# Cross-attention in one core: one doubled column block more, a different order ahead of the batch loop, row loads of 512 KB

## What is computed

```python
qp = x @ Wq + bq; kp = ctx @ Wk + bk; vp = ctx @ Wv + bv
w = softmax(qp @ kp.T / sqrt(512), axis=-1)
a = w @ vp
gate = concat(qp, a) @ Wg + bg
out = (a * mask) * sigmoid(gate) + x
```

## Time and profile before

| | us |
|---|---|
| runs of the kernel (3) | 432.0, 435.47, 435.5 |
| median | 435.47 |
| the profiled execution | 433.39 |
| its span, first to last instruction | 431.5 |

### The profile page before, as it was taken

One profiled execution on the slowest core, in us unless ns is written; L12 is line 12 of the kernel. 1 busy time (PEld: TensorE's weight loads), 2 busy tenths in 40 slices (PEclk: granted clock), 3 DMA queues, 4 the chain that ended last, 5 costly groups with the idle time before them and its releaser, 6 DMA issues.

```text
span 431.5 us, 5269 instructions
## 1 busy us (share of the span) xinstructions
PE 413.2 (96%) x1876; PEld 326.6 (76%) x1876; DVE 224.8 (52%) x386; ACT 154.8 (36%) x267; POOL 126.4 (29%) x98
## 2 busy tenths in 40 slices
PE   7999988999993999999999999999999999999995
PEld 4879966888672777777777777777777777777774
DVE  3786535556541455454554736455454554736453
ACT  4644231234313153332514325153332514325131
POOL 0004135445834050431505234050431505234000
PEclk9999998999999999999999999999999999999999
DMA  7975432468499487769577686867769577685312
GB/s 269 382 295 205 144 83 111 183 193 288 164 268 307 135 261 240 216 218 277 177 238 215 225 252 211 257 197 232 220 210 284 176 239 204 235 254 203 123 50 97
DMA packets 43445, 92.10 MB, mean 213 GB/s; under 512 B 5292, under 2 KB 5292, under 8 KB 42780
## 3 DMA queue, kind: packets, MB, share of 16 engines
q1 hardware_dynamic: 42844, 90.73, 64.9%
q10 hardware_dynamic: 576, 1.05, 0.6%
HBM read 64.75 MB, written 27.00 MB: 213 GB/s over the span
## 4 chain that ended last, share of the span: by engine, by line
PE 87%; DMA 4%; POOL 3%; DVE 2%; ACT 2%; issue 1%; SPq 1%; DVEq 0%
PE bank L425 40%; PE bank L325 29%; PE bank L448 4%; PE bank L449 4%; PE bank L456 3%; PE bank L455 3%; DMA x_raw<-in_xT 3%; PE bank L437 2%; POOL xT L753 1%; POOL wg L753 1%; DMA wqT_raw<-in_wqT 1%; PE bank L395 1%; PE bank L377 1%; POOL v_st L753 0%; DVE ctxT L585 0%
## 5 line engine op out<-in xcount | busy, mean ns | idle before, releaser
L425 PE MATMUL bank<-wqg,xT 128*128 128x512 f32 x768 | 192.2, 396 | 0.0
L425 PEld LDWEIGHTS bank<-wqg,xT 128*128 128x128 f32 x768 | 142.7, 189 | 30.3
L753 POOL TENSOR_TENSOR xT<-x_raw,xT 128x512 fp32r<-128x512 f32 x64 | 87.4, 1396 | 188.6 <-ACT xT L488 188.6
L713 DVE SCALAR_TENSOR_TENSOR prod_sb<-tanh_sb,bank 128x512 f32<-128x512 f32 x64 | 43.9, 686 | 77.7 <-ACT tanh_sb L566 77.7
L566 ACT ACTIVATE tanh_sb<-bank 128x512 f32<-128x512 f32 x64 | 38.3, 599 | 119.8 <-PE bank L449 119.8
L724 DVE SCALAR_TENSOR_TENSOR out_sb<-prod_sb,half_mask,x_rows 128x512 f32<-128x512 f32 x64 | 56.8, 887 | 1.7
L325 PE MATMUL bank<-xT,mt 128*77 128x512 f32 x192 | 47.1, 394 | 0.0
L325 PEld LDWEIGHTS bank<-xT,mt 128*77 128x77 f32 x192 | 27.9, 146 | 15.7
L488 ACT ACTIVATE xT<-x_raw 128x512 fp32r<-128x512 f32 x64 | 35.3, 622 | 5.2 <-DMA x_raw<-in_xT 5.2
L325 PE MATMUL bank<-wg,vT 128*128 128x512 f32 (+1 forms) x120 | 31.0, 408 | 4.5 <-POOL wg L753 3.6
L448 PE MATMUL bank<-v_ext,wT 128*128 128x512 f32 x64 | 26.6, 415 | 5.5 <-ACT wT L554 5.5
(11 more groups left out here) (73 smaller groups left out, 365.7 us busy)
## 6 DMA issues: line engine op xcount, KB each, us to landing
x_raw<-in_xT SPq DMA_DIRECT2D x64, 256.0 KB, 9.7
x_rows<-in_x SPq DMA_DIRECT2D x64, 256.0 KB, 4.9
out_y<-out_sb SPq DMA_DIRECT2D x64, 256.0 KB, 3.5
v_ext<-v_dram SPq DMA_DIRECT2D x32, 308.0 KB
v_dram<-v_st SPq DMA_DIRECT2D x18, 512.0 KB, 3.3
v_ext<-v_dram SPq DMA_DIRECT2D x16, 180.0 KB
ctxT_raw<-in_ctxT SPq DMA_DIRECT2D x4, 624.0 KB, 11.0
ctx_rows<-in_ctx SPq DMA_DIRECT2D x4, 616.0 KB
```

The source lines that it names most:

```text
L425: pe.matmul(gate_ps[n % 3][:, :], xT[b % 2][:, s, c, q], wqg[:, m, c, :], start=(c == 0 and (s, m) == PRODUCTS[0]), stop=False)
L713: dve.scalar_tensor_tensor(prod_sb[:, n % 2, :], tanh_sb[:, n % 2, :], 1.0, attn_ps[n % 2][:, :], ALU.add, ALU.mult).then_inc(prod_made, 1)
L753: pool.tensor_tensor(dst, src, f32(hi_), ALU.subtract).then_inc(made, 1)
```

## The change

1. Doubled columns: prob gets 128 columns; DVE multiplies 32 further ones (L701 has a sibling), the transposes give 128 partitions, ACT copies all of them at once. The first of the two 32-partition copies is gone. `turn_probs` waits for both further multiplies, `low_probs` and the last copy for the one large copy.
2. Shared rests: the rests of wg2 for c = 0 and 2 are made by DVE (ahead of its dot products of pass 1), for c = 1 and 3 by POOL; vg(0) waits for them one by one. ACT splits vT(0) ahead of wg2.
3. Orders: POOL makes the rests of xT(0) two in pass 7 and two in pass 8; exp(0) on ACT and the zeroing of wT and maximum of batch 0 on DVE go ahead of the last tile's vg; in batch 0 ACT copies the probabilities ahead of xT(1).
4. Rows of x: one transfer for two query tiles (512 KB), issued after the store of tiles 1 and 3, where it was one of 256 KB after each store. There are two semaphores a buffer instead of four.

The diff, with little context, without its changes of blank lines and of the list of semaphores (`wT_top` goes, `wg2_lo` becomes two); the number is the line in the kernel before from which a piece begins:

```diff
@@ -107
         expd = sb("expd", D0 + 5952, [P, T, S])
-        prob = sb("prob", D0 + 6272, [P, T, TOP])
+        prob = sb("prob", D0 + 6272, [P, T, P])
         wv = sb("wv", E0, [P, 2, C, D], F32R)
@@ -244
 
-            def load_rows(b, t):
-                sync.dma_start(x_rows[b % 2][:, t, :], x_v[b, t]).then_inc(x_in[b % 2][t], 16)
+            def load_rows(b, h):
+                t = slice(2 * h, 2 * h + 2)
+                sync.dma_start(x_rows[b % 2][:, t, :], x_v[b, t].rearrange("t p d -> p t d")).then_inc(x_in[b % 2][h], 16)
 
@@ -292
                     load_rows(0, 0)
+                if k == 7:
                     load_rows(0, 1)
-                if k == 7:
-                    load_rows(0, 2)
-                    load_rows(0, 3)
             load_vext(1)
...
             sync.wait_ge(dots_made, DOT["sb", 11] + 1)
-            for t in range(T):
-                load_rows(1, t)
+            for h in range(T // 2):
+                load_rows(1, h)
             wait_stored(KT)
@@ -312
                     sync.dma_start(out_v[b, t], out_sb[:, t, :]).then_inc(stored[t], 16)
-                    if b + 2 < B:
-                        load_rows(b + 2, t)
+                    if t % 2 and b + 2 < B:
+                        load_rows(b + 2, t // 2)
             for t in range(T):
@@ -403
                 ps = ps_of(("vg", k - 1))
-                if k == 1:
-                    pe.wait_ge(wg2_lo, C)
                 pe.wait_ge(job_drained, J["vT", k - 1] + 1)
-                for half in range(2):
-                    last = products(ps[0:n, :], lambda s, c: vT[(k - 1) % 2][:, s, c, 0:n], lambda s, c: wg2[:, s, c, :],
-                                    range(half * C // 2, (half + 1) * C // 2))
-                    if half == 0 and k == KT:
+                for c in range(C):
+                    if k == 1:
+                        pe.wait_ge(wg2_lo[c % 2], c // 2 + 1)
+                    if c == C // 2 and k == KT:
                         turn_scores(0)
+                    last = products(ps[0:n, :], lambda s, c: vT[(k - 1) % 2][:, s, c, 0:n], lambda s, c: wg2[:, s, c, :], (c,))
                 last.then_inc(job_done, 1)
@@ -427
                 pe.wait_ge(prob_made, b + 1)
-                pe.wait_ge(prob_twice, b + 1)
+                pe.wait_ge(prob_twice, 2 * (b + 1))
                 if b == 0:
...
                 for t in range(T):
-                    last = pe.transpose(turn_ps[0:TOP, t * P:(t + 1) * P], prob[:, t, :], ident[:, :])
+                    last = pe.transpose(turn_ps[:, t * P:(t + 1) * P], prob[:, t, :], ident[:, :])
                 last.then_inc(turned, 1)
@@ -487
 
+            def exps(b):
+                act.wait_ge(shift_made, b + 1)
+                act.activation(expd[:, :, :], shifted[:, :, :], ACT.Exp, scale=SCALE).then_inc(exp_made, 1)
+
             for c in range(C):
@@ -512
                         hi(wv[:, HI, c], wv_raw[:, c], wv_hi)
+            def vT_hi_of(k):
+                n = KROWS[k]
+                ps = bank[bank_of(J["vT", k])][:, :].rearrange("p (c k) -> p c k", c=C)
+                job_hi_of(("vT", k), vT[k % 2][:, HI, :, 0:n], ps[:, :, 0:n])
+
+            vT_hi_of(0)
             act.wait_ge(wg2_in, 16)
...
             for k in range(KT + 1):
-                if k >= 1:
-                    n = KROWS[k - 1]
-                    ps = bank[bank_of(J["vT", k - 1])][:, :].rearrange("p (c k) -> p c k", c=C)
-                    job_hi_of(("vT", k - 1), vT[(k - 1) % 2][:, HI, :, 0:n], ps[:, :, 0:n])
+                if k >= 2:
+                    vT_hi_of(k - 1)
                 if k < KT:
@@ -529
                     act.wait_ge(dots_made, DOT["sb", 15] + 1)
-                    act.wait_ge(wg2_lo, C)
+                    for i in range(2):
+                        act.wait_ge(wg2_lo[i], C // 2)
                     xT_hi_of(0)
+                if k == KT:
+                    exps(0)
                 if k >= 1:
@@ -538
 
-            def exps(b):
-                act.wait_ge(shift_made, b + 1)
-                act.activation(expd[:, :, :], shifted[:, :, :], ACT.Exp, scale=SCALE).then_inc(exp_made, 1)
-
             def high_probs(b):
...
                     act.wait_ge(attn_done, b * T)
-                act.activation(wT[0:TOP, 0, :], turn_ps[0:TOP, :], ACT.Copy).then_inc(wT_top, 1)
-                act.wait_ge(wT_top, b + 1)
-                act.activation(wT[TOP:P, 0, :], wT[0:Q, 0, :], ACT.Copy).then_inc(wTa_made, 1)
+                act.activation(wT[:, 0, :], turn_ps[:, :], ACT.Copy).then_inc(wTa_made, 1)
+                act.wait_ge(wTa_made, b + 1)
                 act.activation(wT[TOP:P, 1, :], wT[Q:2 * Q, 0, :], ACT.Copy).then_inc(wTb_made, 1)
@@ -565
 
-            exps(0)
             for b in range(B):
                 more = b + 1 < B
+                if b == 0:
+                    high_probs(b)
                 if more:
                     xT_hi_of(b + 1)
-                high_probs(b)
+                if b:
+                    high_probs(b)
                 tanh_tile(b, 0)
@@ -602
                 dve.tensor_scalar(sT[:, :], sT_ps[0:S, :], sb_c[:, b:b + 1], None, ALU.add).then_inc(sT_made, 1)
+
+            def softmax_max(b):
+                sc = score_ps[:, 0:T * S].rearrange("p (t k) -> p t k", t=T)
+                dve.wait_ge(scores_done, b + 1)
+                dve.tensor_reduce(rowmax[:, :], sc, AX.X, ALU.max).then_inc(max_made, 1)
+                dve.wait_ge(max_made, b + 1)
+                dve.tensor_tensor(shifted[:, :, :], sc, rowmax[:, :].unsqueeze(2).broadcast_to([P, T, S]), ALU.subtract).then_inc(shift_made, 1)
 
@@ -657
                     job_lo_of(("vT", k - 1), vT[(k - 1) % 2][:, LO, :, 0:n], ps[:, :, 0:n], vT[(k - 1) % 2][:, HI, :, 0:n])
+                if k == 1:
+                    for c in range(0, C, 2):
+                        lo(wg2[:, LO, c], wg2_raw[:, c], wg2[:, HI, c], wg2_hi, c + 1, wg2_lo[0])
                 if 1 <= k <= B // 2:
@@ -665
                     add_sb(0)
+                    dve.wait_ge(job_done, J["v", KT - 1] + 1)
+                    dve.memset(f32(wT[2 * Q:TOP, 1, :]), 0.0).then_inc(wT_zeroed, 1)
+                    softmax_max(0)
                 if k >= 1:
@@ -682
 
-            def softmax_max(b):
-                sc = score_ps[:, 0:T * S].rearrange("p (t k) -> p t k", t=T)
-                dve.wait_ge(scores_done, b + 1)
-                dve.tensor_reduce(rowmax[:, :], sc, AX.X, ALU.max).then_inc(max_made, 1)
-                dve.wait_ge(max_made, b + 1)
-                dve.tensor_tensor(shifted[:, :, :], sc, rowmax[:, :].unsqueeze(2).broadcast_to([P, T, S]), ALU.subtract).then_inc(shift_made, 1)
-
             def softmax_rest(b):
@@ -699
                 dve.tensor_tensor(prob[:, :, S:TOP], expd[:, :, DUP:S], rinv[:, :].unsqueeze(2).broadcast_to([P, T, TOP - S]), ALU.mult).then_inc(prob_twice, 1)
+                dve.tensor_tensor(prob[:, :, TOP:P], expd[:, :, 0:Q], rinv[:, :].unsqueeze(2).broadcast_to([P, T, Q]), ALU.mult).then_inc(prob_twice, 1)
 
             def low_probs(b):
-                dve.wait_ge(wT_top, b + 1)
+                dve.wait_ge(wTa_made, b + 1)
                 dve.tensor_tensor(wT[0:S, 1, :], turn_ps[0:S, :], f32(wT[0:S, 0, :]), ALU.subtract).then_inc(wT_lo, 1)
@@ -716
                 dve.wait_ge(prod_made, n + 1)
-                dve.wait_ge(x_in[b % 2][t], 16 * (b // 2 + 1))
+                dve.wait_ge(x_in[b % 2][t // 2], 16 * (b // 2 + 1))
                 if b:
@@ -724
 
-            dve.wait_ge(job_done, J["v", KT - 1] + 1)
-            dve.memset(f32(wT[2 * Q:TOP, 1, :]), 0.0).then_inc(wT_zeroed, 1)
-            softmax_max(0)
             softmax_rest(0)
@@ -752
 
-            def xT_lo_of(b):
-                for c in range(C):
+            def xT_lo_of(b, chunks=range(C)):
+                for c in chunks:
                     pool.wait_ge(xT_hi, b * C + c + 1)
@@ -764
                 lo(wv[:, LO, c], wv_raw[:, c], wv[:, HI, c], wv_lo)
-            for c in range(C):
+            for c in range(1, C, 2):
                 pool.wait_ge(wg2_hi, c + 1)
-                lo(wg2[:, LO, c], wg2_raw[:, c], wg2[:, HI, c], wg2_lo)
+                lo(wg2[:, LO, c], wg2_raw[:, c], wg2[:, HI, c], wg2_lo[1])
             for k in range(KT + 1):
...
                     lo(v_st[k % 2][0:n, LO, 0:D], v_f[0:n, :], v_st[k % 2][0:n, HI, 0:D], v_lo)
-                if k == 7:
-                    xT_lo_of(0)
+                if k in (7, 8):
+                    xT_lo_of(0, range((k - 7) * C // 2, (k - 6) * C // 2))
                 if k >= 1:
```

More of the change, by code:

```diff
@@ L159, in build @@
         xT_in = [sem(f"xT_in{c}") for c in range(C)]
-        x_in = [[sem(f"x_in{i}{t}") for t in range(T)] for i in range(2)]
+        x_in = [[sem(f"x_in{i}{h}") for h in range(T // 2)] for i in range(2)]
         stored = [sem(f"stored{t}") for t in range(T)]
@@ L166, in build @@
         ctxT_hi, ctxT_lo = sem("ctxT_hi"), sem("ctxT_lo")
```

(4 more changed lines are left out.)

## The result

The changed kernel took 427.5 us (median of 4 runs, 426.7 to 429.65); the kernel before 435.21 beside it (432.0 to 435.5). The ratio is 0.9852, 95% interval 0.9805 to 0.9898: faster, by 4.4 to 8.5 us. The forecast was 419.5, and its range of 415.0 to 425.5 doesn't hold the result. The profiled execution of the changed kernel is the slowest of its four, 429.65 us with a span of 427.9.

A forecast was written before the change was run, and what follows sets the result against it. TensorE, nearly always at work, was taken as the bound, its few gaps as the gain. Terms 4.6 + 2.8 + 7.4 - 0.3 + 0 = 14.5 us off 433.39 gave 418.9, set at 419.5; range 415.0 to 425.5.

The forecast's parts named there:

- Part 3: Ahead of the loop and in batch 0: new orders win 7.4 us at scores_T(1), bounds 5.5 and 9.4.
- priced that at 0.3: Batch 2's loads leave behind the last store and may reach ACT 0 to 1.4 us late; 0.3 taken as loss.
- TensorE's path to scores_T(1): Batch 0: summed from product times, TensorE would reach scores_T(1) at 135.4 and wait 2.0 us for xT(1)'s rests.
- 1 MB; at 298 GB/s: Ahead of batch 0: store and rows leave in a DMA hole, 3.5 us less queue, of which 1.4 us was taken.
- Part 1: Each batch: doubled columns end the wait at L448, 0.31 us a batch, 4.6 us in all, bounds 0 and 4.7.
- 9 x 0.23: Batch 1: nine products at 0.23 us each from 156.32, so that L448 should start at 158.39 instead of 158.62.
- The rival in which L719 releases TensorE: Each batch: DVE's rest releases TensorE as late as the old copy did, gain nil, 423.5 us; chance 0.07.
- Part 2: Ahead of the loop: shared rests of wg2 win 2.8 us, bounds 1.2 (low clock again) and 4.6.
- the single file: Rests of wg2: DVE and POOL block each other, the four take 4.1 us, gain 0.8 less, 419.7 us; chance 0.08.
- Part 4: Each batch: rows two tiles at a time change nothing, 0; bounds a 0.5 gain and a loss of 1 us a batch.
- The slower rival, rows in front of x_raw: Loop: a 512 KB transfer makes x_raw late and ACT waits in every batch, costing 24 us, 443 us; chance 0.02.
- The rival of the landing: Batch 0: xT(1) lands no earlier or 0.5 later, TensorE's wait brings the lower clock, 422.4 us; chance 0.12.

The follow-up runs named there:

- Part 3 alone: The kernel before with only the new orders ahead of the loop put in: 433.88 us, ratio 0.9984.
- tanh's wait was moved: Changed kernel with tanh and product buffers moved out of the stores' buffers, the wait for stores going from tanh(0) to the first output: 423.21 us.
- The cut load: The 19-row load of each v_ext cut into 16 and 3 rows: 422.13 us in the changed kernel, 427.85 us in the kernel before.
- Part 1 alone: The kernel before with only the doubled columns put in: 431.17 us, ratio 0.9926.
- part 2 alone: The kernel before with only the shared rests of wg2 and vT(0) first put in: 431.64 us, ratio 0.9938.
- the store first: Changed kernel with the last store of vg issued ahead of the five loads of v_ext(1) instead of behind them: 421.73 us.
- all rests on DVE: Changed kernel, last vg store issued earlier, all wg2 rests on DVE, first dot product later: 422.28 us; also with tanh's and SP's store waits moved: 423.34.

## Why the prediction was wrong

**Part 3 is the step that failed**: "What is late next is xT(1) itself ... So the landing sets the time". A second wait was late next: tanh(0), held by the last store until 143.2. Part 3 alone gained 0.5 us, not 7.4. It was there to be read: the wait stands in the code of `tanh_tile`, in the kernel before the store landed at 144.4, 0.1 us ahead of tanh(0), and SP itself waited 9.0 us for it. No idle time of ACT marked it. The prediction saw only that the loads for batch 2 leave behind the last store, and priced that at 0.3. This term was nil in the changed kernel, where ACT waits for no load but xT(1), and came out as the 1.05 us at L447 once tanh's wait was moved.

The landing of xT(1) was mis-sized too, and where a number seems to fit, it is luck. For part 3 by itself the forecast had scores_T(1) at 137.4; it came at 139.48, of which some 1.0 us was lost ahead of the reordered part in that execution (POOL's first rest of xT(0) started at 107.91, not 106.94). For the whole change it had 9 to 11 us earlier, which is 133.8 to 135.8; it came at 137.35, close to 137.4 only by chance. A shorter queue was to bring the landing 1.4 us forward, but from issue to landing the loads took as long as before: the queue gave nothing. And TensorE's path to scores_T(1) leaves out the 1.10 us that the first attention product waits for v_ext(0). TensorE's wait for the rests of xT(1), 1.60 with part 3 alone and 1.71 in the changed kernel against a forecast of 2.0, is what two errors left of each other.

The same step priced the landing by bytes, "1 MB; at 298 GB/s". The cut load shows that bytes were not what held it: with the same bytes, spread, xT(1) landed some 4 us sooner after its issue. The DMA share of 0.99 that I read over 116 to 138 hid this; the tail at 0.06 tells it. The kernel before has this tail too, in a window that the prediction does not use:

```profile
142.00:144.00 2.00, 2.00 (x10) 1.66 (x9) 0.00 (x0) 0.00 (x0) 0.00 (x0) 1.00 0.06 25
```

The Trainium skill, page "DMA: Bandwidth & Descriptors", section "Why a DMA increments its semaphore by 16 and not by 1", says that a transfer runs on the largest number of engines up to 16 that divides both sides' slowest dimension; by it 19 rows run on a single engine. The runs agree: a sixteenth busy in the tail, and 5.4 and 6.6 us won by 16 + 3 rows. Which of the transfers held that engine at each moment the trace doesn't show.

**Part 1 was mis-sized.** I had 0.31 us a batch; the distance of batches fell from 18.50 to 18.34 (scores_T(2) to scores_T(7): 163.31 to 255.81, and 162.47 to 254.16), 0.165 a batch and 2.5 us over 15. The wrong term is "9 x 0.23": behind the transposes the nine products take 2.16 without any wait, not 2.07, so that 2.30 - 2.16 = 0.14 was to be won there, and 0.08 at the second product. The 12 gate products behind gave back 0.05 (2.78 between starts, 2.73 before). Part 1 alone measured 3.35; that this is more than 2.5 stays open, within its interval. The rival in which L719 releases TensorE falls: it ends at 157.28, and the weight load starts at 157.61.

**Part 2 was right in size by the medians**, 2.8 forecast, 2.9 measured alone, but its inner working was slower: the rest of v(0) ended at 67.03 instead of 66.1 and the transposes came at 67.95 instead of 67.2, 0.75 late, close to the 0.8 of the single file. The Trainium skill's rule on this ("SBUF — State Buffer", "Who interferes with whom") agrees with the rows: 1.52 us for DVE's rest beside POOL's, 0.68 alone. What came behind depended on the granted clock. In the profiled executions of the changed kernel and of part 2 alone the 12 products behind the transposes took 4.59 us, and vg(1) started only 1.4 and 1.5 us earlier than before, near the lower bound of 1.2. With the store first they took 3.03 us, vg(1) waited 0.33 us where the forecast had 0.9, and it started at 71.48, 2.7 earlier. So the size fits in an execution at the full clock; that the medians of part 2 alone give 2.9 is not explained by its own trace.

**Part 4** is nothing, as forecast: 0.9991, x_raw landing 10.1 us after its issue in the median (9.7 before) and 12.2 at most. The slower rival, rows in front of x_raw, did not come about; ACT waits for x_raw four times, all for xT(1).

**The rivals and the range.** The rival of the landing was right that xT(1) would land no sooner after its issue and that a landing bounds batch 0, and wrong in which: it watched xT(1) and came to 422.4. The lower clock that it foresaw came behind the wait for tanh. The range let part 3 fall to 5.5 at the least, since I asked only what else could delay xT(1), and not what else the instructions behind the gap wait for. Its fast end was added up wrongly: the upper bounds 4.7 + 4.6 + 8.8 + 0.5 make 18.6 us, not 17.5; the result lies at the other end.

With the measured sizes the sum is 2.5 + 2.9 + 0.5 = 5.9 us, within the 4.4 to 8.5 measured.

## What to carry to other kernels

Before a stall is priced as won, list every semaphore that the next instructions of each engine behind it wait on, waits for a reused buffer included, and look up when each was met: a wait that shows no idle time may have been met 0.1 us ahead. Where the DMA share is near one sixteenth while someone waits, as in 140 to 144 here, look ahead of it for a small transfer with a number of rows like the 19 here, and try cutting it before reordering anything. When a measured time meets a forecast, see that both are of the same set of parts.

## What the runs showed of the hardware

The granted clock differed between executions after the same wait. In the two kernels with all rests on DVE, TensorE waited 2.26 and 2.27 us ahead of vg(1); the 12 products then took 2.97 us in one and, in the other (timeline), 4.47; the granted clock over the 4.5 us from their start was 1.00 and 0.63:

```profile
71.81 4.47 PE L326 MATMUL bank<-wg,vT 128*128 128x512 f32 x12 [2.27 <-DVE vT L592]
```

Likewise 3.03 us with the store first and 4.59 in the changed kernel, both behind waits of 1.59. This stretch alone moves an execution by 1.5 us, which is why the columns above should be compared by differences of several us only.

A DVE multiply of 76 elements a partition, 0.23 us in the loop, took 1.32 in batch 0 of the changed kernel, where it started 0.3 us behind a subtraction on POOL.
